# State-space loop: one product and one scan of 1024 columns per step, and the skip term as a diagonal matmul

## The reference, cut to what matters

```python
x = jnp.einsum('bld,ed->bel', hidden_states, in_proj_w)           # 256 inner channels
x = silu(causal_conv4(x) + conv_b)                                # called u in the kernel
dt_low, Bm, Cm = jnp.split(jnp.einsum('bdl,ed->bel', x, x_proj_w), [8, 24], axis=1)
dt = softplus(jnp.einsum('brl,dr->bdl', dt_low, dt_proj_w) + dt_proj_b)
A = -exp(A_log)                                                   # 256 x 16
def step(state, inp):                                             # over 256 tokens
    d, b, c, u = inp
    dA = exp(d[..., None] * A)
    state = state * dA + (d * u)[..., None] * b[:, None, :]
    return state, einsum('bdn,bn->bd', state, c)
y = y + D[None, :, None] * x                                      # the skip term
y = y * silu(z)                                                   # the gate
```

## Time and profile before

| | |
|---|---|
| runs | 1439.5, 1440.1, 1444.04 us; median 1440.1 |
| profiled execution | 1443.76 us, span 1442.0 us |
| busy in the span | TensorE 1310.5, VectorE 1019.6, ScalarE 706.4, GpSimd 272.7 us |
| start of the first product of the loop | 40.31 us |
| start of the last product of the loop | 158.09 us |
| next layer's first statistics (L347) | 168.61 us |
| mean granted clock of TensorE | 0.95 |

### The profile page before, as it was taken

One profiled execution on the slowest core, in us unless ns is written; L12 is line 12 of the kernel. 1 busy time (PEld: TensorE's weight loads), 2 busy tenths in 40 slices (PEclk: granted clock), 3 DMA queues, 4 the chain that ended last, 5 costly groups with the idle time before them and its releaser, 6 DMA issues.

```text
span 1442.0 us, 20925 instructions
## 1 busy us (share of the span) xinstructions
PE 1310.5 (91%) x6697; PEld 920.2 (64%) x6697; DVE 1019.6 (71%) x2264; ACT 706.4 (49%) x1825; POOL 272.7 (19%) x258
## 2 busy tenths in 40 slices
PE   7898699989996668999999789987999999989998
PEld 3455465663342355766776789976888888765555
DVE  6999877988986877778777522236666666667665
ACT  5797524444774847455554112225666666623110
POOL 0787310010000003222220371111111111201000
PEclk8899889999998879999999699998999999989999
DMA  6579600044502000010105488855222221101330
GB/s 224 169 252 318 206 2 0 0 74 76 89 10 85 0 0 1 1 37 1 37 1 146 168 314 309 305 191 191 74 73 73 74 78 66 36 1 48 82 92 29
DMA packets 83570, 141.80 MB, mean 98 GB/s; under 512 B 45606, under 2 KB 57327, under 8 KB 78528
## 3 DMA queue, kind: packets, MB, share of 16 engines
q1 hardware_dynamic: 80528, 134.44, 29.5%
q0 software_dynamic: 1872, 4.22, 0.8%
q10 hardware_dynamic: 1088, 2.10, 0.4%
HBM read 105.32 MB, written 26.37 MB: 91 GB/s over the span
## 4 chain that ended last, share of the span: by engine, by line
PE 74%; DVE 12%; ACT 5%; issue 3%; DMA 3%; POOL 2%; SPq 1%; DVEq 0%; POOLq 0%; ACTq 0%
PE psum L3363 5%; PE psum L2540 4%; PE psum L2106 4%; PE psum L2860 4%; PE psum L996 4%; PE psum L2912 4%; PE psum L2890 4%; PE psum L2148 4%; PE psum L2925 3%; PE psum L3373 3%; PE psum L603 2%; PE psum L537 2%; DVE roomB L1662 2%; PE psum L2138 2%; PE psum L2551 2%
## 5 line engine op out<-in xcount | busy, mean ns | idle before, releaser
L2982 ACT ACTIVATE roomA<-psum,roomA 128x256 f32<-128x256 f32 x128 | 70.9, 559 | 87.2 <-DVE roomA L3049 86.9
L2203 ACT ACTIVATE roomA<-psum,roomA 128x128 f32<-128x128 f32 (+1 forms) x128 | 53.2, 426 | 84.3 <-DVE roomA L2278 84.2
L1662 DVE TENSOR_REDUCE roomB<-psum 128x2 f32<-128x512 f32 x128 | 81.3, 685 | 10.5 <-PE psum L1501 10.0
L2711 DVE SCALAR_TENSOR_TENSOR roomA<-roomA,psum 128x512 f32<-128x512 f32 x23 | 15.9, 689 | 100.6 <-ACT roomA L2600 100.5
L2069 POOL TENSOR_TENSOR roomA<-roomA 128x512 f32<-128x512 f32 x40 | 51.1, 1279 | 176.6 <-DVE roomA L2271 176.6
L902 POOL TENSOR_TENSOR roomA<-roomA 128x1024 f32<-128x1024 f32 (+1 forms) x33 | 74.8, 2268 | 25.6 <-DVE roomA L822 24.9
L2106 PE MATMUL psum<-own,roomB 128*128 128x512 f32 x160 | 75.0, 594 | 3.4 <-DVE roomA L2270 2.1
L822 DVE TENSOR_TENSOR_SCAN roomA<-roomA,psum 128x512 f32<-128x512 f32 x64 | 74.3, 1200 | 0.9 <-ACT roomA L704 0.9
L3363 PE MATMUL psum<-roomA,roomB 128*112 128x512 f32 (+1 forms) x168 | 74.6, 593 | 0.0
L2912 PE MATMUL psum<-roomA 128*128 128x256 f32 x256 | 67.5, 386 | 1.7 <-ACT roomA L2990 0.7
L2890 PE MATMUL psum<-roomA 128*128 128x256 f32 x256 | 65.6, 379 | 1.7 <-ACT roomA L2982 1.7
(11 more groups left out here) (525 smaller groups left out, 3374.3 us busy)
## 6 DMA issues: line engine op xcount, KB each, us to landing
roomB<-m_w_dram SPq DMA_DIRECT2D x12, 1536.0 KB, 8.2
roomA<-m_w_dram SPq DMA_DIRECT2D x11, 1536.0 KB, 8.8
roomA<-m_c_rows SPq DMA_DIRECT2D x32, 512.0 KB, 4.6
a_kv_ready<-roomB SPq DMA_DIRECT2D x28, 512.0 KB, 5.3
roomA<-a_kv_ready SPq DMA_DIRECT2D x8, 1024.0 KB, 4.9
roomA<-a_kv_ready SPq DMA_DIRECT2D x16, 512.0 KB, 4.3
roomB<-a_w_dram SPq DMA_DIRECT2D x4, 1280.0 KB, 5.6
roomB<-f_w_dram SPq DMA_DIRECT2D x8, 624.0 KB, 4.3
```

The costliest lines, as they stand in the source:

```text
L1662: dve.tensor_reduce(maxneg[:, hp // 8, :, m, hp % 8], g.bank(m).rearrange("p (q k) -> p q k", k=S), AX.X, ALU.max, negate=True).then_inc(s ...
```

## The change

Each step's two products become one `tensor_tensor` over two banks (1024 columns), its two scans one `tensor_tensor_scan` of 1024 columns. `m_products` and `m_scanned` count once a step; both halves of `spread(k + 1)` wait for product k as a whole, the product for both halves of `spread`, the last two `times_c` for the whole scan. `with_skip` goes: VectorE makes two diagonal matrices `skips` once, and at the start of a group TensorE begins the y banks with `skips` times u in fp32 (`skip_over`, two matmuls of 512 columns), ahead of `add`. `gate` reads y straight from PSUM; both gates of group 0 are at k = 17. In the softplus, `logarithm(j)` is Ln with a bias of one on `e` and no longer waits for `one_more`; `remainder` waits for it instead, and `one_more(1)` moves from GpSimd to VectorE (k = 1, after the product). `kv_round(4)` is cut in two halves, one behind `project(1)`, one between `step_size(1)` and `take_off(1)`, and `kv_out(4)` moves behind `logarithm(1)`.

```diff
+        pool.memset(g.one, 1.0)
         pool.memset(g.before, 0.0).then_inc(s["before"], 1)
...
     A = ra.take(E2 * NS)
+    skips = ra.take(E2, P)
     hC = ra.take(2, TOK)
...
         project(0)
-        kv_round(4)
         pe.wait_ge(s["m_u"], 2)
         project(1).then_inc(s["m_dtlow_psum"], 1)
+        kv_round(4, range(0, 2))
         pe.wait_ge(s["m_kv_copied"], 4)
...
         step_size(1)
+        kv_round(4, range(2, 4))
         take_off(1)
...
         def spread(k):
+            if k:
+                pe.wait_ge(s["m_products"], k)
             for half in range(2):
-                if k:
-                    pe.wait_ge(s["m_products"], 2 * k - 1 + half)
                 pe.matmul(g.bank(B_BANK + half), sel[0:96, k % NS, :], bc_parts[0:96, half * HALF:(half + 1) * HALF],
...
+        def skip_over(j):
+            pe.wait_ge(s["m_made"], 4)
+            pe.wait_ge(*((s["m_hc"], 1), (s["m_gated"], 1))[j])
+            for half in range(2):
+                pe.matmul(g.bank(Y_BANK + half), skips[:, j, :], u[:, j, half * HALF:(half + 1) * HALF],
+                          start=True, stop=False, skip_group_check=True)
+
         def add(k):
+            if k % NS == 0:
+                skip_over(k // NS)
             for half in range(2):
                 if k == STEPS - 1 and half:
-                    pe.wait_ge(s["m_products"], 2 * STEPS + 1)
+                    pe.wait_ge(s["m_products"], STEPS + 1)
                 else:
                     pe.wait_ge(s["m_hc"], k + 1 + (half if k == STEPS - 2 else k // (STEPS - 1)))
-                if k == NS:
-                    pe.wait_ge(s["m_gated"], 1)
                 pe.matmul(g.bank(Y_BANK + half), g.ident, hC[:, k % 2, half * HALF:(half + 1) * HALF],
-                          start=(k % NS == 0), stop=(k % NS == NS - 1), skip_group_check=True).then_inc(s["m_added"], 1)
+                          start=False, stop=(k % NS == NS - 1), skip_group_check=True).then_inc(s["m_added"], 1)
         def back(j):
-            pe.wait_ge(s["m_gated"], 2 + j)
+            pe.wait_ge(s["m_gated"], 1 + j)
             for i in range(NT):
                 if j and i == NT // 2:
-                    pe.wait_ge(s["m_gated"], 4)
+                    pe.wait_ge(s["m_gated"], 3)
                 b, r = i // 2, i % 2
...
                 pe.wait_ge(s["m_kv_copied"], ROUNDS)
-                pe.wait_ge(s["m_products"], 2 * STEPS)
+                pe.wait_ge(s["m_products"], STEPS)
                 back(0)
...
         act.activation(A, a_log, ACT.Exp).then_inc(s["m_aexp"], 1)
-        act.wait_ge(s["m_pad"], 2)
+        act.wait_ge(s["m_made"], 2)
         for b in range(4):
...
         kv_out(3)
-        kv_out(4)
         act.preload_act_table_set(LN_EXP)
...
         def logarithm(j):
-            act.wait_ge(s["m_w"], j + 1)
-            act.activation(th[:, j, :], dtu[:, j, :], ACT.Ln).then_inc(s["m_ln"], 1)
+            act.wait_ge(s["m_e"], j + 1)
+            act.activation(th[:, j, :], e[:, j, :], ACT.Ln, bias=g.one).then_inc(s["m_ln"], 1)
...
         split(1)
-        act.wait_ge(s["m_u"], 2)
         logarithm(0)
...
             if k >= 2:
-                act.wait_ge(s["m_scanned"], 2 * (k - 1))
+                act.wait_ge(s["m_scanned"], k - 1)
             if n == 0:
...
         logarithm(1)
+        kv_out(4)
         kv_out(AHEAD - 1)
...
         step = g.dve_steps
-        dve.memset(xpad[:, :, :, 0:TAPS - 1], 0.0).then_inc(s["m_pad"], 1)
+        dve.memset(xpad[:, :, :, 0:TAPS - 1], 0.0).then_inc(s["m_made"], 1)
         dve.wait_ge(s["ident"], 3)
...
         dve.tensor_copy(sel[0:96], ones[0:96, 0:NS].unsqueeze(2).to_broadcast([96, NS, P])).then_inc(s["m_sel"], 1)
-        dve.memset(by_seq(dA[1])[:, :, 0:1], 0.0).then_inc(s["m_pad"], 1)
+        dve.memset(by_seq(dA[1])[:, :, 0:1], 0.0).then_inc(s["m_made"], 1)
         dve.wait_ge(s["m_weights"], 48)
         step(dve.tensor_scalar(small[:, 0:10], small[:, 0:10], 0.5, None, ALU.mult))
+        for j in range(E2):
+            dve.tensor_scalar(skips[:, j, :], g.ident, skip[:, j:j + 1], None, ALU.mult).then_inc(s["m_made"], 1)
...
             dve.wait_ge(s["m_w"], j + 1)
+            dve.wait_ge(s["m_ln"], j + 1)
             return dve.scalar_tensor_tensor(e[:, j, :], dtu[:, j, :], -1.0, e[:, j, :], ALU.add, ALU.subtract)
...
+        two_banks = lambda b: g.ps[:, b * HALF:(b + 2) * HALF]
+
         def inputs(k):
...
                 dve.wait_ge(s["m_second"], 6)
-            for half in range(2):
-                of = slice(half * HALF, (half + 1) * HALF)
-                dve.wait_ge(s["m_b"], 2 * k + half + 1)
-                if k == 0:
-                    dve.wait_ge(s["m_abs"], 2)
-                if k:
-                    dve.wait_ge(s["m_scanned"], 2 * k - 1 + half)
-                dve.tensor_tensor(g.bank(DBU_BANK + half), dtu[:, j, of], g.bank(B_BANK + half), ALU.mult).then_inc(s["m_products"], 1)
+            dve.wait_ge(s["m_b"], 2 * k + 2)
+            if k == 0:
+                dve.wait_ge(s["m_abs"], 2)
+            else:
+                dve.wait_ge(s["m_scanned"], k)
+            dve.tensor_tensor(two_banks(DBU_BANK), dtu[:, j, :], two_banks(B_BANK), ALU.mult).then_inc(s["m_products"], 1)
...
                 dve.wait_ge(s["m_hc"], k - 1)
-            for half in range(2):
-                of = slice(half * HALF, (half + 1) * HALF)
-                dve.wait_ge(s["m_products"], 2 * k + half + 1)
-                dve.tensor_tensor_scan(h[:, k % 2, of], dA[k % 2][:, of], g.bank(DBU_BANK + half), 0.0, ALU.mult, ALU.add)\
-                   .then_inc(s["m_scanned"], 1)
-
-        def with_skip(j, half):
-            of = slice(half * HALF, (half + 1) * HALF)
+            dve.wait_ge(s["m_products"], k + 1)
+            dve.tensor_tensor_scan(h[:, k % 2, :], dA[k % 2], two_banks(DBU_BANK), 0.0, ALU.mult, ALU.add).then_inc(s["m_scanned"], 1)
+
+        def gate(j, half):
             dve.wait_ge(s["m_added"], 2 * NS * (j + 1) - 1 + half)
-            return dve.scalar_tensor_tensor(dtu[:, j, of], u[:, j, of], skip[:, j:j + 1], g.bank(Y_BANK + half), ALU.mult, ALU.add)
-
-        def gate(j, half):
-            y = by_seq(dtu[:, j, :])[:, 2 * half:2 * half + 2, :]
-            return dve.scalar_tensor_tensor(y, gates[:, 2 * half:2 * half + 2, j, :], 0.5, y, ALU.mult, ALU.mult)
+            y = g.bank(Y_BANK + half).rearrange("p (b l) -> p b l", b=2)
+            return dve.scalar_tensor_tensor(by_seq(dtu[:, j, :])[:, 2 * half:2 * half + 2, :], gates[:, 2 * half:2 * half + 2, j, :], 0.5, y,
+                                            ALU.mult, ALU.mult)
...
             if k == 1:
+                one_more(1)
                 remainder(1).then_inc(s["m_w"], 1)
             if k == NS + 1:
-                with_skip(0, 0)
-                with_skip(0, 1).then_inc(s["m_gated"], 1)
+                dve.wait_ge(s["m_gates"], 4)
+                gate(0, 0)
+                gate(0, 1).then_inc(s["m_gated"], 1)
             scan(k)
...
                     normal(i)
-            if k == NS + 2:
-                dve.wait_ge(s["m_gates"], 4)
-                dve.wait_ge(s["m_gated"], 1)
-                gate(0, 0)
-                gate(0, 1).then_inc(s["m_gated"], 1)
         last = slice(HALF, TOK)
-        dve.wait_ge(s["m_scanned"], 2 * STEPS)
+        dve.wait_ge(s["m_scanned"], STEPS)
         dve.wait_ge(s[f"m_c{(STEPS - 1) % 3}"], row_in(STEPS - 1))
...
         for half in range(2):
-            step(with_skip(1, half))
             gate(1, half).then_inc(s["m_gated"], 1)
...
-        def times_c(k, whole, scanned):
-            pool.wait_ge(s["m_scanned"], scanned)
+        def times_c(k, whole):
+            pool.wait_ge(s["m_scanned"], k + 1)
             pool.wait_ge(s[f"m_c{k % 3}"], row_in(k))
...
-        pool.wait_ge(s["m_e"], 2)
-        pool.tensor_scalar(dtu[:, 1, :], e[:, 1, :], 1.0, None, ALU.add).then_inc(s["m_w"], 1)
         for k in range(STEPS):
             if k < STEPS - 2:
-                times_c(k, slice(0, TOK), 2 * k + 2)
+                times_c(k, slice(0, TOK))
             else:
-                times_c(k, slice(0, HALF), 2 * k + 1)
+                times_c(k, slice(0, HALF))
             if k == STEPS - 2:
-                times_c(k, slice(HALF, TOK), 2 * k + 2)
+                times_c(k, slice(HALF, TOK))
             if 2 <= k <= 7:
...
-        own = sb("own", 2 * NT * D + KD * TOK + TOK + P + P // 2 + 240 + 256)
+        own = sb("own", 2 * NT * D + KD * TOK + TOK + P + P // 2 + 240 + 256 + 2)
         g.X = own.take(NT, D)
...
         g.var, g.rstd, g.t8a, g.t8b = (own.take(NT) for _ in range(4))
+        g.one = own.take(1)
         g.roomA = sb("roomA", 25600)
...
         g.late = Room(g.roomB.tensor, 18900)
```

## The result

The changed kernel took a median of 1458.24 us (1454.64 to 1460.12, four runs) against 1440.26 us for the kernel before: a ratio of 1.012 with a 95% interval of 1.0099 to 1.0142. Timed a second time (e5_after_again) it took 1458.71 against 1442.19, 1.0111 (1.0091 to 1.0131). It is slower, as forecast, but by 16 to 18 us and not by 6, and outside the forecast range of 1437.5 to 1451.

The account below looks back on a forecast made before the run. The prediction took a TensorE-ScalarE relay to bound the start-up and VectorE to pace the loop. Start +7.2, loop -1.3 and tail +0.1 sum to +6.0 us; applied to the median 1440.1: 1446.1 us, range 1437.5 to 1451.

Parts of the forecast that it names:

- The start: Start-up: late kv_out(4) holds kv_round(5) ahead of spread(0), so product 0 starts at 47.55 instead of 40.31, +7.2 us.
- The step: VectorE's loop: one whole product and scan, each starting 0.04 past the other's end, take 3.56 us against 3.42.
- The loop's other terms: Loop beside the steps: 3.0 us between product 1 and scan 1, 1.4 for both gates, 1.8 of waits kept.
- The tail: After scan 31: last with_skip pair gone, but the first half comes 1.7 us later; +0.1, between -0.4 and +0.6.
- Rival (b): Loop: the step costs 3.31 by the overlap independent operations show; sum -1.7, 1438.4 us, chance 0.16.
- Rival (a): Start-up: TensorE keeps 2.4 GHz, start +5.0 in place of +7.2; sum +3.8, 1443.9 us, chance 0.13.
- a distance over 119: Loop, product 0 to product 31: 116.5 us was forecast, and over 119 was to show rival (c).
- rival (c): Loop: TensorE becomes the bound through diagonal matmuls and late spread; sum +10.2, 1450.3 us, chance 0.13.

Follow-up runs that it names:

- e5_after_again: The changed kernel, unchanged, timed a second time; 1458.71 us against 1442.19 for the kernel before, ratio 1.0111.
- e8: Kernel before with only the skip term moved: skip_over on TensorE, no with_skip, both gates at k = 17; 1442.47 us against 1442.19, ratio 1.0007.
- e4: Kernel before with only the products and scans widened to 1024 columns; 1449.86 us against 1442.84, ratio 1.0046.
- e12: Kernel of e8 with skip_over(0) behind spread(1) in place of ahead of add(0); 1439.5 us against 1442.76 for the kernel before, ratio 0.9984.
- e2: Changed kernel with kv_round(5) on TensorE behind spread(1) in place of ahead of spread(0); 1455.56 us against 1442.84 for the kernel before, ratio 1.0098.
- e13: Changed kernel with each product's and scan's wait for VectorE's own last operation put first; 1452.45 us against 1441.64 for the kernel before, ratio 1.008.
- e6: Kernel of e2 with SyncE's keep(4) also moved behind the first C rows; 1448.62 us against 1442.19 for the kernel before, ratio 1.0044.
- e7: Kernel of e6 with products and scans back in halves of 512; 1440.4 us against 1442.19 for the kernel before, ratio 0.9991.
- e10: Changed kernel with the 1024-column products written to SBUF and read there by the scans; one run, 1490.6 us.

## Why the prediction was wrong

The direction was right, and so were the wait that holds the start and the dependence that lengthens the step; the sum was mis-sized. The step failed by most: 3.56 was taken and 3.755 measured. The start failed in what it was set against.

**The start (+7.2).** The chain was followed rightly: `kv_out(4)` behind `logarithm(1)`, 8.19 us of stand, 1.2 GHz behind it. The forecast of product 0 in absolute time, 47.55, is close to the two profiles (46.14, 47.73). What failed is what it was set against: 40.31 came from an execution whose kv rounds had waited for the input and whose `step_size(0)` fell mostly behind the drop of the clock; the second of the same kernel starts the loop at 37.91, and e8, e4 and e12, with the same order of the start-up, at 36.22, 37.84 and 39.07. Against 37.91 the term is 8 to 10 us. The prediction marked the state of the clock as a bound of the changed kernel only, not of the one before. It had also missed the second chain, through SyncE's queue, which costs nothing here and 9 us once the first is freed (e2).

**The step (3.56).** Durations as worked out (1.21 and 2.27; measured 1.23 and 2.29). The gap of 0.04 was taken from `L796` and `L797`, where the second waits for its own engine alone; most products have two waits and most scans three, with their own engine's last. 31 x 0.195 = 6.0 us. With the waits reordered the step is 3.58, close to the sum's (e13).

**The loop's other terms (3.0 + 1.4 + 1.8).** Between product 1 and scan 1 lay 2.8 us more than a step's own, the gates cost 1.0, and 0.8 was left of the waits (120.95 - 31 x 3.755 - 2.8 - 1.0): 1.6 us less than taken. That the slower step covers more of the waits is a likely reason and was not tested by itself. The diagonal matmuls fitted in the changed kernel, as said, but only because of that slower step; with halves they cost 2.5 us (e8).

**The tail (+0.1)** was +0.3: the two parts that the prediction named, 1.4 us less without `with_skip` and 1.7 more for the whole scan, both show (e8, and e6 against e7).

Together: 2.4 for the reference profile, 6.0 - 1.6 for the loop, 0.2 for the tail, 7.0 of the 12.1 us between 1446.1 and 1458.24. The other 5 are not traced to a cause: the second profiles, 14.6 us apart, explain 14 of a difference that is 16.5 and 18.0 in the medians, and the median of before was itself 1440.3 to 1442.8 from one comparison to the next.

Rival (b), the step of 3.31, is refuted; by the rule of "VectorE: DVE Perf Modes" in the Trainium skill ("Rules for kernel authors") on the number of operations it should have come out so. The page's section "The DRAIN you can't avoid" reports for a chain of copies that the semaphore costs nothing extra. The trace here does not agree: the second of two halves, which waits for nothing of its own engine that isn't long done, starts 0.08 to 0.09 us before the end of the first, a dependent operation 0.03 us past the end with its own engine's wait first and 0.10 or 0.13 past it with that wait last. Rival (a) held for `step_size(0)` alone (the clock is 1.00 to 28 us, 0.60 from 28 to 30 and 0.50 behind until 45 in the changed kernel), which is what the forecast took. By the prediction's own sign, a distance over 119, rival (c) would have come true; it did not, since only 0.8 us of the 120.95 are waits. The sign could not tell a slower TensorE from a slower step. Rival (c) has a share only in the kernels whose steps are shorter or whose loop starts early.

## What to carry to other kernels

When an instruction is moved back on its engine, look up every wait that counts it, on all queues, the DMA queues too: here one copy held TensorE and SyncE, and freeing one alone won nothing in the layer. Before merging two half operations into one, look at what the next operation depends on: here each kind depends on the other, the halves hide each other's ends, and the merged step was slower even with its waits in the better order. Take a second profile of the kernel before ahead of working out a term of a few us from a start-up in which the clock changes.

## What the runs showed of the hardware that was not expected

- The order of waits in front of a VectorE operation set how soon it started behind its own engine's last one: 0.03 us past the end with the own wait first (e13), 0.10 to 0.11 (two waits) and 0.13 to 0.14 (three) with it last (changed kernel).
- In e10 the scans, now with two SBUF inputs, and GpSimd's products excluded each other: a scan lasted 3.12 us where 0.98 us of a `times_c` were still to run at its start (57.46) and 4.08 where 1.92 were (66.63), against 2.29 with one input in PSUM. GpSimd's half-width products, 1.27 us otherwise, lasted 3.25 beside such a scan. Likewise `one_more(1)`, with one input in SBUF, lasted 1.84 in place of 0.69 beside GpSimd (changed kernel). The Trainium skill says this of the shared port pair, for operations with two SBUF inputs and for those of one input that run at twice the rate (0.69 us for 1024 columns against 1.22) ("SBUF — State Buffer", "Who interferes with whom"), and here the trace agrees for both.
- The same code met the fall of the granted clock at another point from one execution to the next: `step_size(0)` took 3.37 and 1.99 us. With a DMA of the input that came 1.0 us later, that moved the loop's start by 2.4 us.
